# Two layers of a graph network on one core: late products of the moved chunks placed between the last groups of h, a quarter of the last moves on VectorE

## The chip, the cores and the metric

The kernel runs on one core of a Trainium2 chip. The metric is the device time of one execution in microseconds (us), the median of several runs. TensorE (PE in the profile) multiplies, VectorE (DVE), ScalarE (ACT) and GpSimd (POOL) work on elements, and the queue of SyncE (SP) issues the loads of the large matrix.

## The reference, cut to what matters

`x` is 5120 x 64, `adj` is 5120 x 5120 in float32 (105 MB). Both layers end in a layer norm over the 64 features.

```
e   = a * (diag * x) @ W + x                        # per half of the rows
h   = adj @ (adj.T @ e)                             # first layer
y   = layernorm(x + layernorm(h) * gamma + beta + x)
deg = adj.sum(axis=0) + 1;  dinv = rsqrt(deg)
z   = dinv * (y @ W1)
out = relu(dinv * (adj.T @ z + z) + b)              # second layer
out = layernorm(y + out)
```

So `adj` is read twice: once for `t = adj.T @ e` and `h = adj @ t`, block column by block column, and once for `adj.T @ z`. Between the two readings every row of h has to be complete, and the first norm, the projection by W1 and z follow from it.

## The kernel before

**First reading (ten steps).** The matrix is cut into ten block columns J of 512 columns, and a block column into ten chunks of 512 rows, 1 MB each. A step handles one block column. `t_pairs` (matmuls at L827) sums `adj.T @ e` over the ten chunks. VectorE then transposes the chunks in blocks of 32 x 32 in place (`cut_chunk`, L642), and TensorE multiplies them by `t` into h. For the first eight chunks (tiles `slot0` and `slot1`, by turns) this is `h_group` (L932): four groups jb = 0 to 3 of 32 matmuls each. They accumulate the first 4096 rows of h in the four banks `acc`.

The last two chunks of a step lie in `last_slot`. After their transposes, ScalarE and GpSimd move 32-partition pieces of them to the tile `turned`, sixteen copies of 32 x 1024 elements, eight each (`ACT_MOVES` at L446 and `POOL_MOVES` at L395). A pair (a, c) is a move from partition group a to partition group c. `h_last` (L940) multiplies `turned` by t into bank 4, which holds the last 1024 rows of h, called group 4 below: two matmuls for each of the four jb, eight in a step. An fp32 matmul appears as two records in the trace.

**Between the readings.** The 40 row blocks are handled as five groups of eight. For group g, ScalarE copies h out of PSUM (`copy_hT`, L461) and squares it, TensorE turns it with the centring matrix (`turn_h`, L891) and sums the squares (`sum_h`, L903), ScalarE takes the root (`root_h`, L479), VectorE scales and adds the residual (`norm_h`, L698 to L704, which ends in `y_ready`), ScalarE squares y, TensorE transposes it (`turn_y`, L798) and projects it (`project_y`, L990), and VectorE writes z of the group (`norm_y` and `make_z`, L709 to L717). VectorE also transposes the eight chunks of `slot1` back (`restore`, L648), one at a time between these parts.

**Second reading.** The twenty chunks of block columns 0 and 1 are swept first, in the order of the list FIRST (`first_round`, `out_sweep`, matmuls at L827). Sixteen are in `slot0` and `slot1` (`slot0` was loaded again during the last step); the two of q = 8 go to `last_slot`, and the two of q = 9 go to `turned`, since that tile is free after the last `h_last`. Each swept chunk gives its place free for one "wide" load (row block x 2048 columns, 1 MB, L338). There are twenty places, used as a ring, and 80 such loads. `wide_sweep` (L1012) works through them.

**What orders the work.** All orders are written out by hand: each engine's program is a list with waits on semaphores. SP issues in order: the chunks of the last step, then the two `last_slot` loads after all moves, then the two `turned` loads after `h_done` has reached 2 (the last `h_last`), and then wide load n after n+1 sweeps. Everything on SP is behind what stands ahead of it in this list. On TensorE, in the last step, `h_group(3)` raises `h_done` to 1, on which ScalarE's first copy of h and the first `restore` wait. The eight last `h_last` matmuls come after that, two at a time, between the parts of the first norm.

Of the kernel before, what the change touches and what calls it, by code (L numbers as in the profile page):

```python
# [9 lines left out]
JB = JW // P  # L10
# [13 lines left out]
DVE_COPIES = [(a, d) for d in range(1, 4) for a in range(4) if (a + d) % 2 == 0]  # L24
EPS = 1e-5
# [13 lines left out]
def build(nc, x, adj, W_u, diag_u, par_u, W_i, diag_i, par_i, gamma, beta, W1, b1, out):  # L39
# [12 lines left out]
    with ctx:  # L52
# [112 lines left out]
        moved_pool = sem("moved_pool")  # L165
        slots_used = sem("slots_used")
# [117 lines left out]
        def _(sp):  # L284
# [33 lines left out]
            sp.wait_ge(moved_act, NJ * len(ACT_MOVES))  # L318
            sp.wait_ge(moved_pool, NJ * len(POOL_MOVES))
# [3 lines left out]
            sp.wait_ge(h_done, 2)  # L323
# [22 lines left out]
        def _(pool):  # L346
# [43 lines left out]
            for step in range(NJ):  # L390
# [3 lines left out]
                for a, c in POOL_MOVES:  # L394
                    nc.gpsimd.tensor_copy(turned[c * Q32:(c + 1) * Q32, a].rearrange("p h k j r -> p (h k j) r"),  # L395
                                          last_blocks[a * Q32:(a + 1) * Q32, :, c, :]).then_inc(moved_pool, 1)
                    moves += 1
                    pool.wait_ge(moved_pool, moves)
# [15 lines left out]
        def _(act):  # L414
# [25 lines left out]
            def move(step):  # L440
# [4 lines left out]
                for a, c in ACT_MOVES:  # L445
                    nc.scalar.activation(turned[c * Q32:(c + 1) * Q32, a].rearrange("p h k j r -> p (h k j) r"),  # L446
                                         last_blocks[a * Q32:(a + 1) * Q32, :, c, :], ACT.Copy).then_inc(moved_act, 1)
# [8 lines left out]
            def copy_hT(g, n=1):  # L456
                act.wait_ge(h_done, 1 if g < NG - 1 else 2)
                if g == NG - 1:
                    act.wait_ge(h_turned, 1)
# [115 lines left out]
        def _(dve):  # L575
# [94 lines left out]
            for step in range(NJ):  # L670
# [6 lines left out]
                if step == NJ - 1:  # L677
                    sum_degrees()
                if 2 <= step <= NG + 1:
                    centre_residual(step - 2)  # L680
# [110 lines left out]
        def _(pe):  # L791
# [152 lines left out]
            def h_step(step):  # L944
# [11 lines left out]
                h_group(step, 2)  # L956
                h_group(step, 3).then_inc(slots_used if not final else h_done, 1)
# [87 lines left out]
            def last_products(jbs):  # L1045
                for jb in jbs:
                    last = h_last(NJ - 1, jb)
                return last

            pe.wait_ge(moved_act, NJ * len(ACT_MOVES))  # L1050
            pe.wait_ge(moved_pool, NJ * len(POOL_MOVES))
            last_products([0])
            sum_h(0)
            turn_h(0)
            last_products([1])
            turn_y(0)
            last_products([2])
            project_y(0)
            last_products([3]).then_inc(h_done, 1)
            first_round(1)  # L1060
            turn_h(1)
            sum_h(1)
# [63 lines left out]
```

## Time and profile before

| | us |
|---|---|
| median of 3 runs | 618.32 |
| lowest and highest run | 618.21, 619.15 |
| the profiled execution, its own time | 617.02 |
| its span, first to last instruction | 615.3 |
| TensorE busy | 587.3 (95%) |
| VectorE busy | 342.6 (56%) |
| ScalarE busy | 143.3 (23%) |
| GpSimd busy | 108.4 (18%) |
| DMA moved | 204.80 MB, mean 333 GB/s |
| granted TensorE clock, mean | 0.996 |

All positions in the text are microseconds from the start of the profiled span. The last step of the first reading ends near 390, the first sweeps of the second reading run from about 390 to 441, and the wide sweeps from there to 602. The granted clock is 1.0, the 2.4 GHz level, in the stretches discussed. A busy TensorE is not proof that it is the limit: matmuls are pipelined and their ends are modelled.

### The profile page before, as it was taken

How to read it: one execution, taken by the hardware profiler on the slowest of the kernel's cores; microseconds unless marked ns; L12 is line 12 of the kernel's file. 1: busy time of each engine (PE TensorE's matmuls, PEld its weight loads, DVE VectorE, ACT ScalarE, POOL GpSimd, SP SyncE). 2: the span in 40 equal slices, each digit the busy share in tenths (PEclk: the TensorE clock that was granted, in tenths of full speed). 3: DMA queues.
4: the chain of work that ended last, by engine and by line, in shares of the span. 5: the costliest groups of instructions: out<-in, count | busy, mean ns of one | idle time of the engine just before them, and what ended most of it. 6: DMA issues, size and time to landing. Idle time of an engine off the chain costs nothing.

```text
span 615.3 us, 10817 instructions
## 1 busy us (share of the span) xinstructions
PE 587.3 (95%) x4726; PEld 226.5 (37%) x4726; DVE 342.6 (56%) x430; ACT 143.3 (23%) x272; POOL 108.4 (18%) x126
## 2 busy tenths in 40 slices
PE   9989999999999999999999999999999999977794
PEld 6433333333333333333333334454433334222232
DVE  3987666668857667886666783736540003500026
ACT  2015150511506042150604316424100001000001
POOL 3007060330706122050502305010000000000000
PEclk9999999999999999999999999999999999999998
DMA  8999977949777794978869597799999999999993
GB/s 304 387 375 350 332 270 281 386 157 389 266 283 287 264 387 172 374 262 287 308 236 389 197 351 271 263 391 404 399 423 422 421 420 422 422 420 422 414 386 118
DMA packets 77400, 204.80 MB, mean 333 GB/s; under 512 B 4127, under 2 KB 6687, under 8 KB 68137
## 3 DMA queue, kind: packets, MB, share of 16 engines
q1 hardware_dynamic: 76288, 203.27, 87.3%
q10 hardware_dynamic: 1064, 0.84, 0.4%
q8 instruction: 37, 0.61, 0.4%
q14 instruction: 11, 0.08, 0.0%
HBM read 202.79 MB, written 1.31 MB: 332 GB/s over the span
## 4 chain that ended last, share of the span: by engine, by line
PE 79%; DMA 14%; SPq 3%; DVE 2%; ACT 1%; issue 0%; DVEq 0%
PE psum L827 32%; PE psum L932 23%; PE psum L1012 14%; DMA turned<-in_adj_dram 7%; PE psum L940 5%; DMA slot<-in_adj_dram 4%; SPq L286 3%; DMA last_slot<-in_adj_dram 2%; PE psum L869 2%; PE psum L1032 1%; PE psum L891 1%; PE psum L990 1%; PE psum L903 1%; SPq L290 0%; DVE slot L648 0%
## 5 line engine op out<-in xcount | busy, mean ns | idle before, releaser
L642 DVE STREAM_TRANSPOSE slot<-slot 128x2048 f32<-128x2048 f32 x80 | 178.1, 2281 | 75.9 <-PE psum L827 75.9
L827 PE MATMUL psum<-slot,E 128*64 128x512 f32 x800 | 180.0, 597 | 1.2 <-DMA slot<-in_adj_dram 0.8
L932 PE MATMUL psum<-slot,T 32*64 32x512 f32 x2560 | 142.5, 590 | 0.5 <-DVE T L626 0.5
L395 POOL COPY turned<-last_slot 32x1024 f32<-32x1024 f32 x80 | 84.4, 1055 | 273.2 <-DVE last_slot L642 268.9
L1012 PE MATMUL psum<-slot,E 128*64 128x512 f32 x480 | 105.9, 594 | 10.8 <-DMA slot<-in_adj_dram 10.8
L827 PEld LDWEIGHTS psum<-slot,E 128*64 128x64 f32 x800 | 54.4, 137 | 113.7 <-issue 109.6
L446 ACT ACTIVATE turned<-last_slot 32x1024 f32<-32x1024 f32 x80 | 84.3, 1054 | 40.7 <-DVE last_slot L642 38.9
L932 PEld LDWEIGHTS psum<-slot,T 32*64 32x64 f32 x2560 | 54.4, 132 | 85.8 <-issue 81.0
L768 DVE TENSOR_TENSOR T<-psum,dinv 128x256 f32<-128x256 f32 x10 | 4.2, 425 | 134.0 <-PE psum L1032 133.4
L437 ACT ACTIVATE T<-T 32x256 f32<-32x256 f32 x60 | 24.8, 414 | 210.0 <-DVE T L626 208.8
L1012 PEld LDWEIGHTS psum<-slot,E 128*64 128x64 f32 x480 | 35.1, 137 | 78.6 <-issue 78.4
L827 PE MATMUL psum<-last_slot,E 128*64 128x512 f32 x192 | 43.7, 593 | 1.9 <-DMA last_slot<-in_adj_dram 1.9
L642 DVE STREAM_TRANSPOSE last_slot<-last_slot 128x2048 f32<-128x2048 f32 x20 | 45.0, 2290 | 0.3
L547 ACT ACTIVATE turn<-psum 128x512 f32<-128x512 f32 x10 | 5.9, 596 | 145.8 <-PE psum L827 82.6
L940 PE MATMUL psum<-turned,T 128*64 128x512 f32 x160 | 38.7, 600 | 0.0
L827 PEld LDWEIGHTS psum<-last_slot,E 128*64 128x64 f32 x192 | 13.6, 137 | 29.4 <-issue 27.8
L648 DVE STREAM_TRANSPOSE slot<-slot 128x2048 f32<-128x2048 f32 x8 | 18.3, 2300 | 1.7 <-PE psum L932 1.7
L631 DVE COPY T<-T 32x256 f32<-32x256 f32 x60 | 17.1, 284 | 1.9
L940 PEld LDWEIGHTS psum<-turned,T 128*64 128x64 f32 x160 | 10.3, 136 | 17.3 <-issue 16.4
L410 POOL TENSOR_TENSOR X<-X,rstd_y 128x512 f32<-128x512 f32 x5 | 5.2, 1043 | 48.1 <-DVE rstd_y L709 48.1
L869 PEld LDWEIGHTS psum<-fold_t,turn 128*128 128x128 f32 x80 | 9.7, 191 | 9.1 <-DVE turn L621 7.4
L1012 PE MATMUL psum<-turned,E 128*64 128x512 f32 x48 | 10.9, 594 | 1.4 <-DMA turned<-in_adj_dram 1.4
(107 smaller groups left out, 266.9 us busy)
## 6 DMA issues: line engine op xcount, KB each, us to landing
slot<-in_adj_dram SPq DMA_DIRECT2D x152, 1024.0 KB, 14.2
last_slot<-in_adj_dram SPq DMA_DIRECT2D x30, 1024.0 KB, 7.6
turned<-in_adj_dram SPq DMA_DIRECT2D x9, 1024.0 KB, 16.2
X<-in_x_dram SPq DMA_DIRECT2D x5, 256.0 KB, 4.1
turned<-in_adj_dram SPq DMA_DIRECT2D x2, 512.0 KB, 12.1
out_dram<-T ACTq DMA_DIRECT2D x6, 128.0 KB, 7.0
out_dram<-T SPq DMA_DIRECT2D x4, 128.0 KB, 1.8
beta_b<-in_L_gnn_ln_beta_dram SPq DMA_DIRECT2D x1, 32.0 KB, 11.3
```

Source lines behind the costliest of these rows:

```text
L286: sp.dma_start(view, adj_rows[:, q, :, J * JW:(J + 1) * JW]).then_inc(landed, 16)
L395: nc.gpsimd.tensor_copy(turned[c * Q32:(c + 1) * Q32, a].rearrange("p h k j r -> p (h k j) r"), last_blocks[a * Q32:(a + 1) * Q32, :, c, : ...
L437: nc.scalar.activation(T[step % 2][a * Q32:(a + 1) * Q32, :, d, :], T[step % 2][c * Q32:(c + 1) * Q32, :, 0, :], ACT.Copy).then_inc(spread ...
L446: nc.scalar.activation(turned[c * Q32:(c + 1) * Q32, a].rearrange("p h k j r -> p (h k j) r"), last_blocks[a * Q32:(a + 1) * Q32, :, c, :] ...
L631: v.tensor_copy(T[i][a * Q32:(a + 1) * Q32, :, d, :], T[i][c * Q32:(c + 1) * Q32, :, 0, :]).then_inc(spread_dve, 1)
L642: v.transpose(parts, parts).then_inc(chunk_cut, 1)
L648: v.transpose(parts, parts).then_inc(restored, 1)
L827: return mm(acc[half[b % 2], :], E[:, b, :], view[:, b % CB, :], start=(b < 2), stop=(b >= NB - 2))
L869: last = mm(t_turn[:, jb, :], turn[0][:, jb * P:(jb + 1) * P], fold_t[:, :], start=True, stop=True)
L932: last = mm(acc[half[h], a, :], T[step % 2][rows_a, jb, d, :], slot[step % 2][rows_a, h:NF:2, :, cols], start=step == 0 and jb == 0 and d ...
L940: last = mm(bank[4][half[h], :], T[step % 2][:, jb, 0, :], turned[:, :, h, :, jb, :], start=step == 0 and jb == 0, stop=False, skip_group_ ...
L1012: last = mm(bank[ACC[RES + n // NB * WIDE + s]][half[b % 2], :], E[:, b, :], wide[i % PLACES][:, s * JW:(s + 1) * JW], start=(b < 2), stop ...
```

## The change

1. The last step's sixteen moves are divided anew. The four with a = 3 (two of ScalarE's, two of GpSimd's) go to VectorE, which does them after `sum_degrees`. ScalarE and GpSimd keep six each.
2. The last step's eight `h_last` matmuls move from between the parts of the first norm to the place between `h_group(2)` and `h_group(3)`. TensorE waits there for all sixteen moves. A semaphore of their own, `last_done`, releases the `turned` loads on SP and the copy of group 4 on ScalarE, in place of `h_done` at 2.
3. `turn_h(1)` and `sum_h(1)` move ahead: `turn_h(1)` behind `turn_h(0)`, `sum_h(1)` behind `turn_y(0)`. In the order before they stood behind the first sweep.

```diff
+DVE_MOVES = [(a, c) for a, c in ACT_MOVES + POOL_MOVES if a == 3]
+LAST_ACT = [m for m in ACT_MOVES if m not in DVE_MOVES]
+LAST_POOL = [m for m in POOL_MOVES if m not in DVE_MOVES]
+ALL_ACT = (NJ - 1) * len(ACT_MOVES) + len(LAST_ACT)
+ALL_POOL = (NJ - 1) * len(POOL_MOVES) + len(LAST_POOL)
...
-            sp.wait_ge(moved_act, NJ * len(ACT_MOVES))
-            sp.wait_ge(moved_pool, NJ * len(POOL_MOVES))
+            sp.wait_ge(moved_act, ALL_ACT)
+            sp.wait_ge(moved_pool, ALL_POOL)
+            sp.wait_ge(moved_dve, len(DVE_MOVES))
             for s in range(RES):
                 load_first(s, NF)
 
-            sp.wait_ge(h_done, 2)
+            sp.wait_ge(last_done, 1)
             for s in range(RES):
                 load_first(s, NF + 1)
...
-                for a, c in POOL_MOVES:
+                for a, c in POOL_MOVES if step < NJ - 1 else LAST_POOL:
...
-                for a, c in ACT_MOVES:
+                for a, c in ACT_MOVES if step < NJ - 1 else LAST_ACT:
...
             def copy_hT(g, n=1):
-                act.wait_ge(h_done, 1 if g < NG - 1 else 2)
-                if g == NG - 1:
+                if g < NG - 1:
+                    act.wait_ge(h_done, 1)
+                else:
+                    act.wait_ge(last_done, 1)
                     act.wait_ge(h_turned, 1)
...
                 if step == NJ - 1:
                     sum_degrees()
+                    dve.wait_ge(chunk_cut, NJ * NQ)
+                    dve.wait_ge(turned_used, NJ - 1)
+                    for a, c in DVE_MOVES:
+                        v.tensor_copy(turned[c * Q32:(c + 1) * Q32, a].rearrange("p h k j r -> p (h k j) r"),
+                                      last_blocks[a * Q32:(a + 1) * Q32, :, c, :]).then_inc(moved_dve, 1)
...
                 h_group(step, 2)
+                if final:
+                    pe.wait_ge(moved_act, ALL_ACT)
+                    pe.wait_ge(moved_pool, ALL_POOL)
+                    pe.wait_ge(moved_dve, len(DVE_MOVES))
+                    for jb in range(JB):
+                        last = h_last(step, jb)
+                    last.then_inc(last_done, 1)
                 h_group(step, 3).then_inc(slots_used if not final else h_done, 1)
...
-            pe.wait_ge(moved_act, NJ * len(ACT_MOVES))
-            pe.wait_ge(moved_pool, NJ * len(POOL_MOVES))
-            last_products([0])
             sum_h(0)
             turn_h(0)
-            last_products([1])
+            turn_h(1)
             turn_y(0)
-            last_products([2])
+            sum_h(1)
             project_y(0)
-            last_products([3]).then_inc(h_done, 1)
             first_round(1)
-            turn_h(1)
-            sum_h(1)
             first_round(1)
             turn_y(1)
```

The first place is TensorE's order from the last three groups of h to the third sweep. L932 is `h_group`, L940 `h_last`, L903 `sum_h`, L891 `turn_h`, L798 `turn_y`, L990 `project_y` and L827 with `slot` a sweep. This is the order before:

```order
L932 MATMUL psum<-slot,T 64x512 x96
L940 MATMUL psum<-turned,T 64x512 x2
L903 MATMUL psum<-pairs,T 128x2 x4
L891 MATMUL psum<-centre,turn 128x2x64 x4
L940 MATMUL psum<-turned,T 64x512 x2
L798 MATMUL psum<-ident,X 128x128 x4
L940 MATMUL psum<-turned,T 64x512 x2
L990 MATMUL psum<-W_out,xT 128x128 x4
L940 MATMUL psum<-turned,T 64x512 x2
L827 MATMUL psum<-slot,E 64x512 x4
L891 MATMUL psum<-centre,turn 128x2x64 x4
L903 MATMUL psum<-pairs,T 128x2 x4
```

After those rows come a sweep, `turn_y(1)` and another sweep. This is the same stretch of the changed kernel, where the new line numbers are L948 for `h_group`, L956 for `h_last`, L919 for `sum_h`, L907 for `turn_h`, L814 for `turn_y`, L1013 for `project_y` and L843 for a sweep:

```order
L948 MATMUL psum<-slot,T 64x512 x64
L956 MATMUL psum<-turned,T 64x512 x8
L948 MATMUL psum<-slot,T 64x512 x32
L919 MATMUL psum<-pairs,T 128x2 x4
L907 MATMUL psum<-centre,turn 128x2x64 x8
L814 MATMUL psum<-ident,X 128x128 x4
L919 MATMUL psum<-pairs,T 128x2 x4
L1013 MATMUL psum<-W_out,xT 128x128 x4
L843 MATMUL psum<-slot,E 64x512 x8
L814 MATMUL psum<-ident,X 128x128 x4
L843 MATMUL psum<-slot,E 64x512 x4
```

All eight `h_last` matmuls now stand ahead of the last 32 of `h_group`, and the places that they left are taken by the second group's turning and sum.

The second place is VectorE between the last transposes of `last_slot` (L653 in the changed kernel) and the first `restore` (L659):

```order
L653 STREAM_TRANSPOSE last_slot<-last_slot 128x2048 x2
L664 TENSOR_SCALAR scale<-psum 128x4x8
L665 TENSOR_SCALAR scale<-psum 128x4x2
L666 TENSOR_SCALAR dinv<-scale 128x40
L693 COPY turned<-last_slot 32x1024 x4
L704 TENSOR_SCALAR scale<-scale 128x40
```

The four copies (L693) are new; the rows around them are the ones that stood there before.

## Rows read from the trace of the kernel before

**Rows 1.** The page, busy shares in 40 equal slices: what the DMA moved

```profile
GB/s 304 387 375 350 332 270 281 386 157 389 266 283 287 264 387 172 374 262 287 308 236 389 197 351 271 263 391 404 399 423 422 421 420 422 422 420 422 414 386 118
```

**Rows 2.** Stretches: PE, PEld, DVE, ACT, POOL busy us (instructions); clock, DMA share, GB/s

```profile
390.40:405.75 15.35, 14.95 (x86) 7.82 (x88) 8.76 (x13) 4.38 (x22) 1.47 (x2) 1.00 0.94 359
405.75:427.15 21.40, 21.40 (x122) 10.57 (x120) 9.74 (x16) 7.47 (x40) 2.09 (x2) 1.00 1.00 389
427.15:434.53 7.38, 7.19 (x38) 3.02 (x36) 6.47 (x8) 2.91 (x18) 1.04 (x1) 1.00 0.99 399
450.00:580.00 130.00, 117.87 (x556) 41.89 (x554) 17.07 (x80) 3.77 (x9) 0.00 (x0) 1.00 1.01 422
```

**Rows 3.** Timeline of SP's queue: start us, us, the loads issued

```profile
379.65 1.22 SPq L286 DMA_DIRECT2D last_slot<-in_adj_dram  x2
...
390.40 1.21 SPq L286 DMA_DIRECT2D turned<-in_adj_dram  x2
...
392.60 0.34 SPq L338 DMA_DIRECT2D slot<-in_adj_dram  x1
...
402.00 0.33 SPq L338 DMA_DIRECT2D slot<-in_adj_dram  x1
...
405.75 0.33 SPq L338 DMA_DIRECT2D slot<-in_adj_dram  x1
...
427.15 2.04 SPq L338 DMA_DIRECT2D slot<-in_adj_dram  x2
```

**Rows 4.** The chain that ended last, in order of time: start us, us, what

```profile
371.54 10.48 PE psum L932 x192
...
390.62 1.94 PE psum L827 x8
392.56 1.09 PE psum L891 x8
393.65 0.80 PE psum L903 x8
...
396.48 0.66 PE psum L798 x4
...
446.72 68.82 PE psum L1012 x320
```

**Rows 5.** Timeline, the last step's moves and VectorE beside them

```profile
370.79 8.61 ACT L446 ACTIVATE turned<-last_slot 32x1024 f32<-32x1024 f32 x8 [3.89 <-DVE last_slot L642]
370.88 8.70 POOL L395 COPY turned<-last_slot 32x1024 f32<-32x1024 f32 x8 [27.50 <-DVE last_slot L642]
...
372.03 1.02 DVE L655 TENSOR_SCALAR dinv<-scale 128x40 f32<-128x40 f32 x1
...
379.69 0.18 DVE L688 TENSOR_SCALAR scale<-scale 128x40 f32<-128x40 f32 x1 [6.64 <-ACT dinv L454]
```

**Rows 6.** Timeline of the third step: GpSimd's moves beside a VectorE operation

```profile
117.49 9.05 POOL L395 COPY turned<-last_slot 32x1024 f32<-32x1024 f32 x8 [24.57 <-DVE last_slot L642]
...
117.97 1.09 DVE L662 SCALAR_TENSOR_TENSOR X<-rsum,X 128x512 f32<-128x512 f32 x1
```

**Rows 7.** VectorE by line, shapes apart: busy us, mean ns of one

```profile
L631 DVE COPY T<-T 32x256 f32<-32x256 f32 x60 | 17.1, 284 | 1.9
...
L704 DVE TENSOR_TENSOR X<-C,X 128x512 f32<-128x512 f32 x5 | 3.5, 692 | 0.2
```

**Rows 8.** Timeline of the first norm: TensorE's gaps and VectorE

```profile
386.59 0.66 PE L798 MATMUL psum<-ident,X 128*128 128x128 f32 x4 [0.57 <-DVE X L704]
...
387.18 1.08 PE L940 MATMUL psum<-turned,T 128*64 128x512 f32 x4
...
388.19 1.16 PE L990 MATMUL psum<-W_out,xT 128*128 128x128 f32 x8
...
390.49 2.30 DVE L648 STREAM_TRANSPOSE slot<-slot 128x2048 f32<-128x2048 f32 x1
...
394.77 0.20 DVE L698 RECIPROCAL rstd_h<-std_h 128x8 f32<-128x8 f32 x1 [1.99 <-ACT std_h L479]
```

More of the change, by code:

```diff
@@ L165, in build @@
         moved_pool = sem("moved_pool")
+        moved_dve = sem("moved_dve")
+        last_done = sem("last_done")
         slots_used = sem("slots_used")
@@ L1043, in first_round @@
                     swept.append((s, q))
[L1045 to L1048, printed above, removed]
-            pe.wait_ge(moved_act, NJ * len(ACT_MOVES))
-            pe.wait_ge(moved_pool, NJ * len(POOL_MOVES))
-            last_products([0])
             sum_h(0)
             turn_h(0)
-            last_products([1])
+            turn_h(1)
             turn_y(0)
-            last_products([2])
+            sum_h(1)
             project_y(0)
-            last_products([3]).then_inc(h_done, 1)
             first_round(1)
-            turn_h(1)
-            sum_h(1)
             first_round(1)
```

## The prediction

> **What bounds the kernel now.** I read the page's slices first. From the 30th slice to the end of the 37th (446 to 569) the DMA moves a steady 420 to 423 GB/s; in the three slices ahead (400 to 446) it moves 391 to 404 [rows 1]. A stretch of the full phase gives 422 GB/s with TensorE busy 117.87 of 130 us [rows 2]. So the second reading is bound by the transfers, and the end of the kernel comes a fixed amount of work after the last moment at which the DMA ran short. The chain of waits doesn't say so outright: it charges 68.82 us of this phase to TensorE [rows 4], because each load waits for a sweep. The question is who sets the start of the full phase.
>
> I answered it with a balance of the queue. A load is 1.049 MB, that is 2.49 us at 422 GB/s. From 390.40 to 405.75 six loads are issued (two `turned` ones, four wide ones, the last at 402.00) [rows 3], 6.29 MB, and 359 GB/s x 15.35 us = 5.51 MB are moved [rows 2]. At 405.75, when the fifth wide load is issued, 0.78 MB is left: 1.85 us of work. At full rate these bytes need 13.1 us if all move at 422, and 13.5 if the two `turned` loads move at 387, as loads of their kind do in full slices of the first reading (the 2nd, 8th and 10th, 386 to 389 [rows 1]). So 1.8 to 2.3 us, say 2.1, went between the first issue and its data at full rate. A queue that holds less than 2.1 us of work when the next load is issued is about to run dry. From 405.75 to 427.15 eight more loads are issued and 389 x 21.4 = 8.32 MB moved: 0.85 MB, 2.0 us, is left when the pair at 427.15 is issued. Three loads later, at 434.53, 399 x 7.38 = 2.94 MB are gone, and 2.5 us is left. After this, sweeps come every 1.72 us (eight records of 68.82/320 = 0.215 us [rows 4]) against 2.49 us for a load, and the queue only grows. So at about 406, at 427 and nearly at 434 the DMA is fed just in time by TensorE's sweeps. **What sets the time is when TensorE gets through the first sweeps**; transfers issued before them pay only while they are in their way.
>
> **The change, part by part.** The sum is for the profiled execution (617.02, span 615.3, 1.7 around it). It lies 1.3 below the median, and I put the difference on the median.
>
> *The wait for the moves.* The groups of `h_group` take 10.48/3 = 3.49 us, so group 2 ends at 371.54 + 6.99 = 378.53 [rows 4]. ScalarE's six moves end at 370.79 + 6/8 x 8.61 = 377.25, GpSimd's at 370.88 + 6/8 x 8.70 = 377.41 if nothing stops them [rows 5]. VectorE starts its four when L655 ends, at 373.05. Their shape is not in the trace. One copy of a quarter of the elements takes 0.284 us [rows 7]; four times that, 1.14 us, is the upper bound of one, 0.28 the lower, and I take the middle, 0.7. Alone, VectorE ends between 374.2 and 377.6, ahead of 378.53.
>
> But it is not alone. L655 has 40 elements a partition, as has L688, which takes 0.18 us. L655, issued while GpSimd ran its second move, took 1.02 and ended when that move did (370.88 + 2/8 x 8.70 = 373.06) [rows 5]. In the third step, L662 started half-way through a move, took 1.09 us where an operation of 512 elements takes 0.692 [rows 7], and GpSimd's eight moves took 9.05 instead of 8.70 [rows 5, 6]. The two engines stop each other. With one meeting costing GpSimd 0.35 us, and four copies meeting its moves 3 to 6, its last move ends at 377.41 + 1.4 = 378.8, and VectorE's last copy, by turns with it, by 379.0. TensorE then waits 0.3 to 0.5 us after group 2: I take +0.45. Bounds: 0 (no meeting counts), and 380.2 - 378.5 = +1.7 (all four copies added whole, 4 x 0.7 = 2.8). Behind this wait on TensorE stand the eight `h_last`, group 3 and with it everything else; SP's `last_slot` loads go out at about 379.1 instead of 379.65.
>
> This is the lock that the Trainium skill describes (SBUF — State Buffer, section Who interferes with whom): a VectorE copy of this kind and a GpSimd instruction exclude each other for the whole instruction. The trace agrees in kind. By the page the sum could come out at the end where each copy blocks GpSimd for its whole length, which is the last rival below.
>
> *`h_last` ahead of group 3.* Sixteen records of 0.215 us: +3.44 us before `h_done` [rows 4]. Nothing hides it, since TensorE has no gap there (up to +3.6 if changing tile shapes costs something). Before, these matmuls lay in gaps: ahead of the one pair TensorE came to 386.59 with a wait for VectorE left, and the pair at 387.18 stood in the wait for the transposed y, which ended at 388.19 [rows 8]. Taking them out of there gains nothing by itself. `h_done` comes at +3.9.
>
> *The second group's turning in those gaps.* `turn_h(1)` takes 1.09 us, as long as a pair of `h_last` (1.08). Such a pair stood ahead of `turn_y(0)`, and TensorE still waited 0.57 us there; `sum_h(1)` takes 0.80, less than the 1.0 us between 387.18 and 388.19. So both are free there, and the first sweep follows `h_done` at the same distance: +3.9, at 394.5. Gone from behind the first sweep are 1.09 + 0.80 us [rows 4]. The next point that waits is `turn_y(1)`, at 396.48 before. It needs `norm_h(1)`: before, VectorE waited 1.99 us for its root until 394.77 [rows 8]. Now the root is there early, and VectorE is late instead, busy with `restore(2)` from 390.49 to about 392.75 (+3.9). From the reciprocal to `turn_y(1)` it is 396.48 - 394.77 = 1.71 us, so `turn_y(1)` can come at 394.46 + 3.9 against 396.48: 2.02 us won. TensorE's two sweeps (2 x 1.72 us from 390.62) are done 0.4 earlier, so they don't limit.
>
> *Sum on TensorE:* 0.45 + 3.44 - 2.02 = **+1.9 us** from the third sweep on. The order of TensorE, VectorE and ScalarE after it is unchanged and TensorE is busy throughout 405.75 to 427.15 [rows 2], so all later sweeps and all later issues keep this +1.9.
>
> *The `turned` loads.* They are issued at 378.53 + 0.45 + 3.44 = 382.4 instead of 390.40, and fill an idle stretch: the pair issued at 379.65 needs 2.1 + 5.2 us, until 387.0, and nothing is issued until 390.40 [rows 3]. That takes 5.2 us of transfer out of the way of the first wide load. But this one goes out at 392.60 + 3.9 = 396.5, its data flows from 398.6, against 390.40 + 2.1 + 5.2 = 397.7 before (two loads, 2.097 MB at an estimated 404 GB/s, between 387 and 422). Even here the stream starts 0.9 us later, and the fifth wide load, issued at 407.65, finds the queue dry (four loads from 398.6 end at 408.6, its data comes at 409.75). The early loads are worth nothing at the end.
>
> *From TensorE to the end.* What was left in the queue beyond the 2.1 us at the tight points is what the delay can use up: 0 at 405.75 and 427.15, 0.4 at 434.53. I take 0.2 as the cushion, since the 2.1 comes from loads in small pieces and no row shows it for wide ones. So **+1.7 us**: 617.0 becomes 618.7, and the median 618.32 becomes 620.0. The last output blocks follow the last load as before.
>
> **The rivals.**
>
> *The queue absorbs it.* If wide loads need much less than 2.1 us to start, the queue never ran dry at 406 or 427, and there is up to 1 to 1.8 us of cushion. For it: the DMA share is 1.00 from 405.75 to 427.15 [rows 2]. Against: the rate there is 389, not 422. Then only the start of the stream counts (+0.9) or less: 1.9 less 1.0 to 1.8 gives +0.1 to +0.9, about 618.8.
>
> *Not slower.* At 389 and 399 GB/s the DMA lost 21.4 x (1 - 389/422) = 1.7 and 0.4 us there. No row shows the cause. If the loss belongs to how these transfers meet and not to the supply, shifting them can remove it: 1.7 - 2.1 = -0.4, 617.9. It decides once more than 1.7 us come back; for more than 0.2% faster 2.9 would have to. Against it: the queue gets thinner, not fuller.
>
> *The lock costs its whole length.* The copies add 2.8 us to GpSimd's moves, TensorE waits 1.7 instead of 0.45: +3.0, 621.3. For it: L655 waited for nearly a whole move. Against: the meeting in the third step cost GpSimd half a copy.
>
> That VectorE's share doesn't shorten the moves at all is the middle of this: they end at 379.5 as before, +1.0 instead of 0.45.
>
> **How the numbers follow.** The forecast (+1.1 to +2.3) gets 50%, absorbed 22%, not slower 15%, the whole lock 13%. 0.2% is 1.24 us, about what a measurement of this kernel can tell from no change. Slower by more than that: most of the forecast (42%) and the last rival, 55%. Within: 8% of the forecast, nearly all of absorbed (20%), a third of the third case (5%), 33%. Faster: the rest, 12%. The range 617.8 to 621.2 leaves out about half of "not slower" and half of the whole lock.
>
> **What the changed kernel's profile would show.** VectorE's four copies from 373.05, each 0.7 us alone and over 1 us where it meets a GpSimd move, GpSimd's six taking about 7.9 instead of 6.5 us; `h_last` starting near 379.0, sixteen records, no gap to group 3, which ends at 385.9; `turned` loads at 382.4; the first sweep at 394.5; `turn_y(1)` at 398.4; the fifth wide load at 407.65; a DMA idle stretch between about 391.5 and 398.5; the last load landing near 603.7. The prediction is wrong if TensorE's shift at `turn_y(1)` is not near 1.9, or if the rate between 407 and 436 changes.

## The result, and the profile after

The changed kernel takes 621.05 us (median of 20 runs, 619.35 to 624.99); the kernel before, in 20 runs beside it, 617.91 (617.2 to 619.15). The ratio is 1.0052, with a 95% interval of 1.0039 to 1.0066: the change makes the kernel 0.5% slower, by about 3.1 us, where 1.7 were forecast. The median lies 0.15 us inside the upper end of the forecast range. Already here something stands out: the runs of the changed kernel spread over 5.6 us, those of before over 2.

The profiled execution took 619.89 us, span 618.2. Its page, what the DMA moved in each slice (compare [rows 1]):

```profile
GB/s 302 387 374 354 332 264 285 380 166 391 261 289 265 283 387 162 392 262 285 274 275 387 160 388 285 227 355 398 401 423 421 421 422 420 423 421 422 412 386 109
```

The full phase begins in the same slice and has the same rate; the 26th and 27th slices moved less (227 and 355, before 263 and 391). The timeline around the last moves (compare [rows 5]): start us, us, engine, line.

```profile
370.77 6.46 ACT L455 ACTIVATE turned<-last_slot 32x1024 f32<-32x1024 f32 x6 [3.88 <-DVE last_slot L653]
...
370.85 7.57 POOL L404 COPY turned<-last_slot 32x1024 f32<-32x1024 f32 x6 [27.48 <-DVE last_slot L653]
...
373.06 5.91 DVE L693 COPY turned<-last_slot 32x1024 f32<-32x1024 f32 x4
...
379.11 3.65 PE L956 MATMUL psum<-turned,T 128*64 128x512 f32 x16 [0.56 <-DVE turned L693]
382.70 3.69 PE L948 MATMUL psum<-slot,T 32*64 32x512 f32 x64
```

VectorE's four copies start every 1.48 us, not every 0.7, and GpSimd's six moves take 7.57 us instead of 6.5: the two engines go by turns. TensorE waits 0.56 us for them. The timeline further on, TensorE's waits and the first sweeps (compare [rows 8]):

```profile
387.14 1.05 PE L919 MATMUL psum<-pairs,T 128*128 128x2 f32 x8 [0.76 <-ACT T L478]
...
390.78 0.66 PE L814 MATMUL psum<-ident,X 128*128 128x128 f32 x4 [0.69 <-DVE X L720]
...
394.82 3.65 PE L843 MATMUL psum<-slot,E 128*64 128x512 f32 x16 [1.30 <-DVE E L733]
398.57 0.66 PE L814 MATMUL psum<-ident,X 128*128 128x128 f32 x4
```

`turn_y(1)` stands at 398.57, 2.09 us after before's 396.48 [rows 4]. SP's queue (compare [rows 3]) and the stretches (compare [rows 2]):

```profile
379.05 1.21 SPq L294 DMA_DIRECT2D last_slot<-in_adj_dram  x2
382.80 1.21 SPq L294 DMA_DIRECT2D turned<-in_adj_dram  x2
```

```profile
407.84:429.24 21.40, 21.40 (x122) 10.57 (x120) 9.75 (x15) 7.51 (x40) 2.09 (x2) 1.00 0.98 387
429.24:436.62 7.38, 7.19 (x38) 3.02 (x36) 6.47 (x8) 2.93 (x18) 1.04 (x1) 1.00 0.92 340
450.00:580.00 130.00, 118.41 (x556) 41.91 (x552) 18.65 (x89) 4.08 (x10) 0.00 (x0) 1.00 1.01 422
```

Between the same two sweeps as before the DMA moves as much in the first stretch (387 GB/s against 389) and less in the second (340 against 399); the full phase is the same. TensorE's shift is the one that was forecast. What is not there is the missing 1 to 1.5 us, and this profile's clock is full in the stretches shown here, so it can't show a cause that only other executions have.

### The profile page after: what moved, and what is told of

Read it like the earlier page. It is cut to its first block, busy times and chain, and to the rows that moved or that the text cites. A ratio compares the mean times of both kernels' runs of the same rounds, so it can differ in the third digit from the quotient of the medians.

```text
span 618.2 us, 10818 instructions
## 1 busy us (share of the span) xinstructions
PE 586.7 (95%) x4726; PEld 226.9 (37%) x4726; DVE 348.4 (56%) x434; ACT 141.4 (23%) x270; POOL 107.6 (17%) x124
## 4 chain that ended last, share of the span: by engine, by line
PE 78%; DMA 14%; DVE 3%; SPq 3%; ACT 1%; issue 1%; DVEq 0%
PE psum L843 31%; PE psum L948 22%; PE psum L1035 14%; DMA turned<-in_adj_dram 7%; PE psum L956 6%; DMA slot<-in_adj_dram 4%; SPq L294 3%; DMA last_slot<-in_adj_dram 2%; PE psum L885 2%; PE psum L1055 1%; DVE turned L693 1%; DVE slot L659 1%; PE psum L1013 1%; PE psum L907 1%; PE psum L919 1%
## 5 line engine op out<-in xcount | busy, mean ns | idle before, releaser
L653 DVE STREAM_TRANSPOSE slot<-slot 128x2048 f32<-128x2048 f32 x80 | 178.1, 2282 | 76.0 <-PE psum L843 76.0
L843 PE MATMUL psum<-slot,E 128*64 128x512 f32 x800 | 179.7, 597 | 2.3 <-DVE E L733 1.3
L948 PE MATMUL psum<-slot,T 32*64 32x512 f32 x2560 | 142.8, 591 | 0.5 <-DVE T L637 0.5
L843 PEld LDWEIGHTS psum<-slot,E 128*64 128x64 f32 x800 | 54.4, 137 | 114.6 <-issue 110.1
L455 ACT ACTIVATE turned<-last_slot 32x1024 f32<-32x1024 f32 x78 | 82.4, 1056 | 40.5 <-DVE last_slot L653 38.8
L948 PEld LDWEIGHTS psum<-slot,T 32*64 32x64 f32 x2560 | 54.2, 132 | 86.1 <-issue 81.3
L843 PE MATMUL psum<-last_slot,E 128*64 128x512 f32 x192 | 43.7, 594 | 2.0 <-DMA last_slot<-in_adj_dram 2.0
L653 DVE STREAM_TRANSPOSE last_slot<-last_slot 128x2048 f32<-128x2048 f32 x20 | 45.0, 2290 | 0.3
L956 PE MATMUL psum<-turned,T 128*64 128x512 f32 x160 | 38.1, 598 | 0.6 <-DVE turned L693 0.6
L843 PEld LDWEIGHTS psum<-last_slot,E 128*64 128x64 f32 x192 | 13.6, 137 | 29.4 <-issue 27.8
L659 DVE STREAM_TRANSPOSE slot<-slot 128x2048 f32<-128x2048 f32 x8 | 18.3, 2301 | 6.7 <-PE psum L948 6.7
L956 PEld LDWEIGHTS psum<-turned,T 128*64 128x64 f32 x160 | 10.8, 136 | 19.0 <-issue 18.4
L1035 PE MATMUL psum<-last_slot,E 128*64 128x512 f32 x48 | 10.9, 594 | 1.3 <-DMA last_slot<-in_adj_dram 1.3
```

The lines of the kernel that those rows point to most:

```text
L653: v.transpose(parts, parts).then_inc(chunk_cut, 1)
L659: v.transpose(parts, parts).then_inc(restored, 1)
L843: return mm(acc[half[b % 2], :], E[:, b, :], view[:, b % CB, :], start=(b < 2), stop=(b >= NB - 2))
L948: last = mm(acc[half[h], a, :], T[step % 2][rows_a, jb, d, :], slot[step % 2][rows_a, h:NF:2, :, cols], start=step == 0 and jb == 0 and d ...
L956: last = mm(bank[4][half[h], :], T[step % 2][:, jb, 0, :], turned[:, :, h, :, jb, :], start=step == 0 and jb == 0, stop=False, skip_group_ ...
L1035: last = mm(bank[ACC[RES + n // NB * WIDE + s]][half[b % 2], :], E[:, b, :], wide[i % PLACES][:, s * JW:(s + 1) * JW], start=(b < 2), stop ...
```

## The experiments

Twelve runs were made, in three sets of four; each set was timed beside the kernel before on one chip, a different chip for each set. Executions differ upstream by up to 3 us (the degree products of the last step start between 369.44 and 372.45), so positions below are counted from them. This table of positions, worked out from one trace of each run, is the main instrument: "to turn_y(1)" is that distance, and "to the last data" the distance to the sweep that waited for the last load. The numbers in brackets are the shifts against before. The text also counts "low" runs, those with a mean granted clock below 0.994; of the kernel before it is known for the 77 runs of the three sets, and 12 are low.

| kernel | to turn_y(1) | to the last data | median, before in its set |
|---|---|---|---|
| before | 26.40 | 231.97 | |
| changed | 28.52 (+2.12) | 234.88 (+2.91) | 621.05, 617.91 |
| turn_back | 33.97 (+7.57) | 240.46 (+8.49) | 625.04, 618.44 |
| delay | 29.30 (+2.90) | 235.72 (+3.75) | 621.83, 618.44 |
| quarter_late | 25.94 (-0.46) | 231.79 (-0.18) | 618.0, 618.44 |
| split_763 | 27.91 (+1.51) | 234.06 (+2.09) | 620.34, 618.44 |
| turn_back_fill | 33.37 (+6.97) | 239.73 (+7.76) | 627.11, 618.93 |
| after_fill | 29.29 (+2.89) | 235.05 (+3.08) | 621.86, 618.93 |
| split_763_fill | 28.68 (+2.28) | 235.25 (+3.28) | 619.76, 618.93 |
| turned_late | 28.49 (+2.09) | 234.60 (+2.63) | 621.94, 618.93 |
| before_gaps | 28.57 (+2.17) | 235.01 (+3.04) | 619.41, 618.00 |
| after_again | 29.97 (+3.57) | 236.24 (+4.27) | 621.79, 618.00 |
| after_fill2 | 28.52 (+2.12) | 235.07 (+3.10) | 619.79, 618.00 |
| three_763 | 27.24 (+0.84) | 233.42 (+1.45) | 620.02, 618.00 |

From `turn_y(1)` to the last data it takes 205.57 us in the profile of before and 205.76 to 206.57 in the thirteen others, 206.27 on average, over shifts from -0.5 to +7.6. So the end follows TensorE's arrival at the sweeps one for one, and there is no cushion. The third column's shifts are a further 0.2 to 1.0 us larger than the second's: they are taken against before's distance of 205.57, the shortest of the fourteen. That this is the scatter of one execution is likely, but no second profile of before shows it.

**turn_back**: the second group's turning behind the first sweep again.

```diff
             turn_h(0)
-            turn_h(1)
             turn_y(0)
-            sum_h(1)
             project_y(0)
             first_round(1)
+            turn_h(1)
+            sum_h(1)
             first_round(1)
```

> The changed kernel with the second group's turning and sum put back behind the first sweep; h_last stays ahead of group 3. Theory (TensorE's arrival at the sweeps feeds the DMA, which then ends as much later): the first sweep stays at about 394.8, turn_y(1) moves from 398.57 to about 400.7, so TensorE is 4.2 us behind the kernel before, 2.1 behind the changed one, and the median is 2 to 3 us above the changed kernel's, 623 to 624. Rival (the queue's thin start, not TensorE, sets the end): the wide stream starts where it does in the changed kernel, so the time is as there, 621.

Measured: 625.04 us (5 runs), ratio 1.0119 [1.0100, 1.0138]. Slower than even the theory had it. The stretches, with the granted clock before the last two columns:

```profile
382.00:386.00 4.00, 3.98 (x66) 1.30 (x64) 0.00 (x0) 0.00 (x0) 0.00 (x0) 1.00 1.04 396
386.00:390.00 4.00, 2.05 (x16) 1.86 (x16) 3.47 (x4) 3.27 (x6) 0.00 (x0) 1.00 1.05 387
390.00:394.00 4.00, 2.95 (x12) 2.42 (x12) 2.90 (x4) 2.91 (x18) 0.30 (x1) 0.56 0.37 134
394.00:398.00 4.00, 3.15 (x9) 0.77 (x8) 2.91 (x2) 0.00 (x0) 0.75 (x1) 0.50 0.00 0
398.00:402.00 4.00, 4.00 (x22) 3.07 (x22) 0.10 (x1) 0.40 (x2) 0.00 (x0) 0.66 0.57 188
```

TensorE was busy 2.05 of 4 us, and then the clock fell to 0.50, the 1.2 GHz level, for about 10 us: one sweep took 3.68 us instead of 1.94. This is where a second cause came into view: **waits on TensorE can cost it its clock**. The changed kernel has more of them than before, though fewer than this one. Of the shift of 7.57 us the order was expected to make 4.2; the half-speed stretch is what the trace shows for the rest.

**delay**: the kernel before with pure delay ahead of group 3.

```diff
+                if final:
+                    for i in range(5):
+                        mm(bank[7][half[i % 2], :], E[:, i, :], slot[step % 2][:, 0, i % CB, :],
+                           start=True, stop=True)
                 h_group(step, 3).then_inc(slots_used if not final else h_done, 1)
```

> The kernel before with five extra fp32 matmuls of 64 x 512 into a free bank between group 2 and group 3 of h in the last step (no part of the result uses them): ten records, 2.15 us of TensorE work, nothing else moved, and the turned loads stay where they were. Theory: everything from group 3 on is 2.2 to 2.4 us later, turn_y(1) at 398.7 to 398.9, as in the changed kernel, and the time is 2.2 to 2.4 above before if delay alone counts; if the DMA's further loss of 0.8 seen in the changed kernel comes from the delay too, 3.0 to 3.2. Rival (the extra loss belongs to the turned loads' early place): 2.2 to 2.4 here, with the rate from 427 to 434 as before. Rival (the queue has a cushion of 1 us or more): at most 1.3.

Measured: 621.83 (6 runs), ratio 1.0068 [1.0053, 1.0083]. The ten records took 2.72 us, not 2.15, so the dose was 2.9, and the time rose by 3.4. The rival with a cushion of 1 us is out. The ratio, 4.2 us, lies above the dose, and a part of this is not from the first norm: three of the six runs are low although the pairs of `h_last` stand in the waits here as before, and the profiled execution has its clock at 1.00 from 378 to 430 but at 0.91 between 30 and 50 us, in the first step (the last section has the row). It is also out that the early place of the turned loads is needed for the loss: here they kept their place.

**quarter_late**: the changed kernel with a quarter of the last `h_last`; its h is incomplete.

```diff
-                    for jb in range(JB):
-                        last = h_last(step, jb)
-                    last.then_inc(last_done, 1)
+                    h_last(step, JB - 1).then_inc(last_done, 1)
```

> The changed kernel with only one of the four pairs of h_last in the last step (the last 1024 rows of h lack three quarters of their last contribution); all else as changed. TensorE has 2.58 us less before group 3. Theory: turn_y(1) at about 396.0, 0.4 to 0.5 us ahead of the kernel before, and the time is within 0.5 us of before, 617.4 to 617.9. Rival (the early turned loads themselves cost, or the moves on VectorE do, by a way not seen on TensorE): still 1 us or more above before.

Measured: 618.0 (12 runs) against 618.44, ratio 0.9995 [0.9981, 1.0010]. With 2.6 us of products out of the way all of the change's cost is gone. The moves on VectorE and the early turned loads cost nothing of their own that this can tell. The runs fall into two clumps, six at 616.5 to 617.4, none of them low, and six at 618.6 to 619.7, five of them low: the changed kernel's waits (0.76, 0.69 and 1.29 us) are open here too.

**split_763**: three moves on VectorE, seven on ScalarE.

```diff
-DVE_MOVES = [(a, c) for a, c in ACT_MOVES + POOL_MOVES if a == 3]
+DVE_MOVES = [(3, 0), (3, 1), (3, 3)]
```

> The changed kernel with three moves on VectorE, seven on ScalarE and six on GpSimd, in place of 4, 6 and 6. ScalarE ends at 370.77 + 7 x 1.076 = 378.3; GpSimd, met by three copies, at 370.85 + 6.5 + 3 x 0.35 = 378.4; VectorE at 377.5. Group 2 ends at 378.5. Theory: the wait of 0.56 us ahead of h_last is gone, all behind it is 0.5 to 0.6 earlier, and the time is 0.5 to 0.6 below the changed kernel's, near 620.5. Rival (the wait is hidden by something later): no difference to the changed kernel.

Measured: 620.34 (11 runs) against 618.44, ratio 1.0026 [1.0012, 1.0039]. The wait is gone from the trace, `turn_y(1)` is 0.61 earlier, and the median is 1.2 us nearer to before than the changed kernel's, on another chip. GpSimd's six moves took as long beside three copies as beside four, 7.57 us: in both kernels its last three take 1.38 to 1.39 us each, where the others take 1.04. Here they are:

```profile
373.67 1.39 POOL L404 COPY turned<-last_slot 32x1024 f32<-32x1024 f32 x1
...
375.12 1.38 POOL L404 COPY turned<-last_slot 32x1024 f32<-32x1024 f32 x1
...
376.56 1.39 POOL L404 COPY turned<-last_slot 32x1024 f32<-32x1024 f32 x1
```

In the changed kernel the fourth copy runs on past GpSimd's last move, to 378.97, and this end is what TensorE waited for.

**turn_back_fill** and **after_fill**: the waits filled with products that nothing uses, nine and five of them. The edit's start:

```diff
+            def fill(n, to):
+                pe.wait_ge(slot_loaded[0][0], NJ // 2 * 16 + 16)
+                if to == 1:
+                    pe.wait_ge(hT_ready, copies(NG - 2))
+                for _ in range(n):
+                    mm(bank[to][half[0], 64:512], ident[:, 0:F], slot[0][:, 0, 0, 0:448], start=True, stop=True)
+
+            fill(1, 7)
             sum_h(0)
...
```

> As turn_back, with TensorE's waits between group 3 and the first sweep filled by nine fp32 matmuls of 448 columns into free banks, 0.38 us each, whose results are never used: one before sum_h(0), three before turn_y(0), two before project_y(0), three before the first sweep. In turn_back the granted clock fell to 0.5 from 390.7 to about 401, after a stretch (386 to 390) in which TensorE was busy 2.05 of 4 us, and all five runs had a mean clock of 0.986 to 0.990. Theory (gaps in TensorE's work let the clock fall, and the half-speed stretch costs 3 to 4 us): with the gaps filled the clock stays at 1.0 there, every run shows 0.994 or more, and the median falls from 625.0 to 621.5 to 622.5. Rival (the low clock comes from something else, the time is all order): clock and time stay as in turn_back.

Measured: 627.11 (5 runs), ratio 1.0124 [1.0102, 1.0146]: by its ratio no better than turn_back, where 3 us less were expected. In the first norm the clock did stay, 1.00 from 380 to 410, and the mean clocks are 0.991 to 0.998 against 0.986 to 0.990; but the profiled execution has the fall in the first step (0.91 between 30 and 50), and its last step starts 2.4 us later than before's. The nine fillers were also too heavy. The three ahead of `turn_y(0)` began only when the copies of h were done, and ran into the chain; the first sweep came 26.8 us after the degree products against 25.4 in turn_back. What the clock gave, the filling took, at least in part. It says nothing on the size.

> The changed kernel with its waits filled in the same way by five such matmuls: one before sum_h(0), one before turn_y(0), three before the first sweep, each in a wait that is long enough, so nothing is delayed by more than 0.1 us. Twelve of the changed kernel's twenty runs had a mean clock below 0.994 and a median of 622.2, the other eight 619.8. Theory: nearly all runs now show 0.994 or more, the median is 619.5 to 620.0, and the scatter shrinks. Rival (the low-clock runs have another cause): half of the runs stay low and the median at 621.

Measured: 621.86 (6 runs), ratio 1.0052 [1.0031, 1.0072]. The filling moved `turn_y(1)` by 0.8, so the median says little. But the theory had nearly all runs at 0.994 or more, and three of six were low, although TensorE was busy throughout 386 to 398 in the profile and its clock stayed: this expectation failed.

**split_763_fill**: both edits.

> The changed kernel with the 7/6/3 division of the last moves and the same five filling matmuls. Theory: both effects add, 0.6 us from the wait that is gone and the clock kept: 619.0 to 619.4, still about 1 us above the median of before since h_last ahead of group 3 remains. Rival (the order costs nothing beyond wait and clock): equal to before, 618.1.

Measured: 619.76 (12 runs) against 618.93, ratio 1.0020 [1.0006, 1.0034]; three of twelve runs low. Here too the filling cost 0.8 at `turn_y(1)`, so the two effects can't be added up from it.

**turned_late**: the turned loads issued ten microseconds later.

```diff
-            sp.wait_ge(last_done, 1)
+            sp.wait_ge(yT_ready, 1)
             for s in range(RES):
                 load_first(s, NF + 1)
```

> The changed kernel with the two turned loads held until the first transposed y is copied (yT_ready at 1), so issued at about 392.4 in place of 382.8, nothing else moved. Theory (early turned loads are worth nothing at the end): their data ends at 392.4 + 2.1 + 5.2 = 399.7, the four wide loads after it at 409.7, and the fifth wide load's data comes at 409.9 anyway: no difference to the changed kernel, within 0.5 us. Rival (the early place of the turned loads is worth the idle stretch it fills): 1 us or more slower than the changed kernel. Rival (their early place costs, through what the DMA then meets): faster.

Measured: 621.94 (11 runs) against 618.93, ratio 1.0040 [1.0024, 1.0057]. Issued at 392.57 in place of 382.80, with the same distances (28.49 and 234.60 against 28.52 and 234.88), and the time is the changed kernel's within the noise.

```profile
392.57 1.21 SPq L294 DMA_DIRECT2D turned<-in_adj_dram  x2
```

**The early loads, the one thing that the new order gives the DMA, are worth nothing**. These eleven runs fall apart by the clock: four at 619.05 to 619.86 with 0.995 or more, seven at 621.25 to 623.43 and low.

**before_gaps**: the kernel before with three late pairs left out and nothing in their place; its h is incomplete.

```diff
-            last_products([0])
             sum_h(0)
             turn_h(0)
-            last_products([1])
             turn_y(0)
-            last_products([2])
             project_y(0)
```

> The kernel before with three of its four late pairs of h_last left out (the last 1024 rows of h lack three quarters of their last contribution), those that stood ahead of sum_h(0), turn_y(0) and project_y(0); the fourth, with the release of the turned loads, stays. The pairs lay in waits, so positions on TensorE hardly move (turn_y(1) at 396.2 to 396.5) and its waits grow by 2.6 us between 382 and 389. Theory (emptier stretches make the granted clock fall in more executions): half of the runs or more have a mean clock below 0.994, against a fifth to a quarter of the kernel before's, and the median rises by 0.5 to 1.5 us although work was taken away. Rival (the gaps do nothing to the clock): low-clock runs as rare as before, time equal or 0.2 us less.

Measured: 619.41 (12 runs) against 618.00, ratio 1.0018 [1.0006, 1.0030]. **With work taken away the kernel is 1.4 us slower.** Seven of twelve runs were low, against 2 of the 32 runs of before beside it and 12 of all 77. Its stretches:

```profile
382.00:386.00 4.00, 2.08 (x17) 1.92 (x18) 3.48 (x5) 2.84 (x7) 0.00 (x0) 1.00 1.05 404
386.00:390.00 4.00, 3.24 (x14) 2.44 (x16) 2.78 (x4) 2.72 (x18) 0.86 (x1) 0.54 0.07 26
390.00:394.00 4.00, 4.00 (x12) 0.90 (x8) 2.61 (x2) 0.00 (x0) 0.18 (x1) 0.61 0.25 47
```

and the first two of them in before:

```profile
382.00:386.00 4.00, 4.00 (x27) 2.21 (x24) 3.24 (x4) 3.28 (x6) 0.00 (x0) 1.00 1.04 398
386.00:390.00 4.00, 3.43 (x22) 1.78 (x20) 3.25 (x5) 2.80 (x18) 0.21 (x1) 1.00 0.26 94
```

Up to the fall every position, counted from the degree products, is before's within 0.05 us (`turn_y(0)` 16.50 us behind them, before 16.51); only the waits are emptier. The pairs were not free fill in the waits: they kept the clock up in most executions.

**after_again**: the changed kernel once more.

> The changed kernel once more beside the kernel before on the same chip, to compare runs at full clock with runs at full clock (mean clock of 0.994 or more in both) and the shares of low-clock runs. Theory: full against full +2.0 us (TensorE's shift at turn_y(1)), more than half of the changed kernel's runs low, all runs together +3. Rival (order alone makes the whole 3 us): full against full +3 and the shares equal.

Measured: 621.79 (9 runs) against 618.00, ratio 1.0052 [1.0035, 1.0070]. This time the profiled execution has the fall in it. The stretches, and TensorE's timeline:

```profile
386.00:390.00 4.00, 3.24 (x32) 2.75 (x24) 3.06 (x3) 3.27 (x6) 0.00 (x0) 1.00 1.02 371
390.00:394.00 4.00, 2.73 (x22) 2.33 (x20) 3.25 (x5) 3.18 (x20) 0.00 (x0) 1.00 0.50 188
394.00:398.00 4.00, 3.16 (x8) 1.00 (x10) 3.90 (x6) 0.29 (x1) 1.04 (x1) 0.59 0.00 0
```

```profile
394.84 5.28 PE L843 MATMUL psum<-slot,E 128*64 128x512 f32 x16 [1.29 <-DVE E L733]
400.05 0.66 PE L814 MATMUL psum<-ident,X 128*128 128x128 f32 x4
```

The first two sweeps take 5.28 us instead of 3.65, `turn_y(1)` comes 1.45 later than in the first profile, and everything behind it too. TensorE's busy times in these stretches are within 0.05 us of those of the first profile of the changed kernel, where the clock stayed:

```profile
386.00:390.00 4.00, 3.24 (x32) 2.75 (x24) 3.09 (x3) 3.28 (x6) 0.00 (x0) 1.00 1.05 387
390.00:394.00 4.00, 2.69 (x21) 2.33 (x20) 3.25 (x4) 3.21 (x20) 0.02 (x1) 1.00 0.51 187
394.00:398.00 4.00, 3.18 (x16) 1.06 (x16) 3.90 (x6) 0.28 (x1) 1.03 (x1) 1.00 0.16 31
```

The same gaps bring the fall in one execution and not in another. Full clock against full clock the four runs at 0.994 or more gave +3.2, the rival's number and not the theory's 2.0. It doesn't decide: 0.995 is this execution's mean clock, fall included, so the mean over 620 us misses a fall of 4 us. In the first comparison the same sorting gave 619.79 for the eight runs at 0.994 or more and 622.2 for the twelve low ones. The shares differ widely, against the rival: 17 of the changed kernel's 29 runs were low.

**after_fill2**: the changed kernel with lighter filling, one product of 192 columns before `sum_h(0)`, one before `turn_y(0)`, two of 448 before the first sweep.

```diff
+            fill(1, 7, 192)
             sum_h(0)
             turn_h(0)
             turn_h(1)
+            fill(1, 1, 192)
             turn_y(0)
             sum_h(1)
             project_y(0)
+            fill(2, 1, 448)
             first_round(1)
```

> The changed kernel with lighter filling than after_fill, which itself delayed turn_y(1) by 0.8 us: one fp32 matmul of 192 columns before sum_h(0), one before turn_y(0), two of 448 before the first sweep; results unused. Theory: turn_y(1) within 0.2 us of the changed kernel's place counted from its last step, a quarter of the runs or fewer at low clock, median 619.5 to 620.5 where the changed kernel has 621 to 621.9. Rival: the share of low-clock runs stays above a half.

Measured: 619.79 (12 runs), ratio 1.0026 [1.0011, 1.0041]; two of twelve runs low. In its trace:

```profile
386.00:390.00 4.00, 3.71 (x41) 2.83 (x26) 2.87 (x3) 3.12 (x6) 0.00 (x0) 1.00 1.03 378
390.00:394.00 4.00, 3.65 (x26) 2.83 (x26) 3.29 (x4) 3.15 (x21) 0.00 (x0) 1.00 0.54 201
394.00:398.00 4.00, 4.00 (x18) 2.22 (x18) 3.90 (x6) 0.48 (x1) 1.04 (x1) 1.00 0.02 4
```

This is the run that comes nearest to separating the two causes. `turn_y(1)` is exactly where the changed kernel's first profile has it, four useless products are added, and the median falls by 2.0 us, from 621.79 to 619.79 on the same chip. With nine and twelve runs this fall is known only roughly (the two ratios, 1.0052 and 1.0026, say 1.6 us, and their intervals touch), and it is more than the 1.45 us that one fall of the clock cost `turn_y(1)` in after_again. What remains against before, 1.8 us, agrees with the 2.1 of the order.

**three_763**: 7/6/3, and the fourth pair of `h_last` between group 3 and `sum_h(0)`.

```diff
-                    for jb in range(JB):
-                        last = h_last(step, jb)
-                    last.then_inc(last_done, 1)
+                    for jb in range(JB - 1):
+                        h_last(step, jb)
...
+            h_last(NJ - 1, JB - 1).then_inc(last_done, 1)
             sum_h(0)
```

> The changed kernel with the moves divided 7/6/3 and only three of the four pairs of h_last ahead of group 3; the fourth stands between group 3 and sum_h(0), in the wait for ScalarE's square, and releases the turned loads there. Theory: without the wait, and with 0.9 us less ahead of h_done, turn_y(1) comes 0.8 to 1.0 us after before's place (26.4 us from the last step's degree products), and the time is 0.8 to 1.0 above before. Rival (the fourth pair delays sum_h(0) by its own length): +1.5 and more.

Measured: 620.02 (11 runs) against 618.00, ratio 1.0017 [1.0002, 1.0031]. `turn_y(1)` came at +0.84 as expected. The medians say +2.0, the ratio +1.1; only one run of eleven was low, although the waits of 0.69 and 1.30 us are open here and only the one ahead of `sum_h(0)` is filled. Why the median lies above the trace's shift is open. One candidate is in its own profile: the clock is at 0.91 between 30 and 50 us, the last step starts 2.0 us later than before's, and the mean clock still reads 0.994. How often that happens in either version isn't known. No complete version of the new order beat the kernel before.

## Why the prediction was right, and where it was short

- **What bounds the kernel**: right. The end is tied to TensorE's arrival at the first sweeps, 205.6 to 206.6 us ahead of the last data, in fourteen profiles.
- **The wait for the moves**: forecast +0.45, measured +0.56. GpSimd took 7.57 us for six moves (7.9 forecast): the 0.35 us for a meeting, taken from the third step, is right, but only three of its moves were lengthened, not four. VectorE's end at 378.97 (379.0) is as forecast. The Trainium skill (SBUF — State Buffer, section Who interferes with whom) says the loser blocks until the winner's whole instruction is done; the trace agrees in that the copies follow each other by 1.48 us, each ending some 0.5 us after a move's end. The rival that gave each of four copies 0.7 us of GpSimd's time is refuted by its number: 1.05 us in all. No copy runs alone in a trace, so whether 0.35 us is less than a whole copy isn't shown.
- **`h_last` ahead of group 3**: forecast +3.44, measured 3.59 (379.11 to 382.70), within the bound of 3.6. Group 3 ends at 386.39, 4.4 us after before's 382.01, where the sum had 3.9 at this point. Of the 0.5 the wait is 0.1 and `h_last` 0.15; the rest is in no term of the sum. In delay and three_763 group 3 takes 3.62 us up to the next matmul when it follows other products, and 3.50 when it follows group 2, which gives another 0.1.
- **The turning in the gaps**: forecast -2.02, measured -2.3 (group 3 ends 4.4 later, `turn_y(1)` 2.09 later). `sum_h(0)` also came 0.2 sooner after group 3's end, now that no pair stands ahead of it. So the +2.1 is near the +1.9 partly because one miss, +0.5, was made good by another, -0.3.
- **Sum on TensorE**: +1.9 forecast, +2.1 measured.
- **The turned loads**: worth nothing, as forecast; shown by turned_late.
- **From TensorE to the end**: I took a cushion of 0.2. There is none. The prediction named a changed rate between 407 and 436 as a sign that it is wrong, and the rate did change, from 399 to 340 GB/s between 429 and 437. The sign was ill chosen: the same stretch, counted from `turn_y(1)`, moves between 340 and 416 GB/s in the fourteen profiles, and the distance to the last data doesn't follow it (351 and 402 GB/s go with 206.18 and 206.27 us).
- **The step that fell short** is one that the sum lacks. The prediction treated TensorE's waits in the first norm as neutral ("Taking them out of there gains nothing by itself"), having priced only the work moved out of them. What stood in those waits was work that kept the clock at 2.4 GHz, as before_gaps shows. In the changed kernel TensorE's busy time between 390 and 394 is 2.7 of 4 us, and in a part of the executions the clock is at half for some 4 us from 395. after_fill2 puts this at 2.0 us of the 3.8 in its set; in the first comparison, with 3.1, it is about 1, if the order makes 2.1. The Trainium skill describes such a loss (TensorE: Matmul & The Clock Gate, section HAM oscillation — how this bites in real kernels) for a loop whose waits for DMA are longer than its matmuls: the work behind the wait starts at half the clock. The trace of after_again agrees in this, 5.28 us for two sweeps instead of 3.65, but its waits, 0.76, 0.69 and 1.29 us, are shorter than the work between them. I had the clock of 1.00 in the rows of before and didn't ask what held it there.
- **How sure the second cause is**: counting the runs, 46 of 80 are low in the versions with open waits (the changed kernel, turn_back, split_763, turned_late, quarter_late, before_gaps), 10 of 35 in the four with filling, 12 of 77 in before. Two versions don't fit, delay (3 of 6 low with the waits filled) and three_763 (1 of 11 with most of them open), and a low mean also counts falls in the first step. That open waits can cost the clock is shown by before_gaps; how the 3.1 us divide between order and clock is known only roughly.
- **Right in part by luck**: the bracket of the forecast was +1.1 to +2.3, and +3.1 lies outside it. It is the number of the whole lock (+3.0), of whose 1.7 us of wait only 0.56 were there. What was right is the direction and TensorE's shift.
- **Rivals**: the absorbing queue is refuted (delay, turn_back), "not slower" too (the distance is never below before's), and the whole lock by 0.56 us of wait, where it had 1.7.

Of the 1.3 us by which the profiled execution of before lay under its median some 0.7 turned up again in the table: its last stretch, 205.57 us, is the shortest of fourteen, and the others average 206.27. A forecast made against one such execution inherits its luck.

## What to carry to other kernels

Small products that stood in TensorE's waits cost nothing where they were (before_gaps moved nothing forward) and were not idle cargo: before moving them out, ask what TensorE will be busy with there, and if nothing, whether the work behind the wait can afford half the clock. Where a stream of transfers is fed just in time by one engine, count first how late that engine arrives; the transfers that were pulled ahead of the stream here only filled a hole that was there anyway. And when runs of one version scatter more than those of the other, the reason may be missing from the one profile at hand: run the version again before trusting its trace.

## What the runs showed of the hardware

- The same order with the same gaps (TensorE busy 3.24 of 4 us, then 2.7 of 4) kept the full clock in one profiled execution and fell to 0.5 from 394.9 to 398.9 in another. With 2.05 or 2.08 of 4 us it fell in the two profiled executions that had it, for about 10 and 7 us.
- A second place has it, in kernels of either order: three profiles of fourteen (delay, turn_back_fill, three_763) show a mean clock of 0.91 between 30 and 50 us, in the first step, and their last step starts 1.2 to 2.4 us later than before's. The row of delay:

```profile
30.00:50.00 20.00, 17.88 (x174) 6.73 (x172) 15.03 (x15) 5.72 (x10) 3.05 (x3) 0.91 1.05 378
```

- Ten fp32 records of 512 columns that followed `h_group` took 2.72 us, 0.27 each, in delay, where a long row of them takes 0.215; group 3 behind them took 3.62 us up to the next matmul, where it takes 3.50 behind group 2.
